# Halves of the K and Q projections placed singly between transposes and products of a batch step

## The reference

```python
x = x + xattn(layernorm(x), ctx, ctx, Wq, Wk, Wv, Wo, bo, g)   # x, ctx: (32, 64, 512)
x = x + ffn(layernorm(x), c1_w, c2_w, w1, w2t)

def xattn(q, k, v, ...):              # per batch, 8 heads of 64
    qh = softmax(Wq q, over the 64 channels of a head) * 64 ** -0.5
    kh = softmax(Wk k, over the 512 positions)
    context = kh vh^T                 # 64 x 64 per head
    out = context^T qh ; out = Wo out + bo ; out = out / norm * g * sqrt(64)

def ffn(x, c1_w, c2_w, w1, w2t):      # per row
    inter = x c1^T c2^T ; per block of 32 of the 1792: idx = argmax
    h = relu(w1[idx] . x) ; out = h w2t[idx]
```

## Time and profile before

| | us |
|---|---|
| median of 3 runs | 860.18 |
| lowest, highest | 857.99, 1524.28 |
| the profiled execution | 858.17 |
| its span, first to last instruction | 856.3 |

### The profile page before, as it was taken

How to read it: one execution, slowest core, us unless ns; L and a number is a source line. 1 busy time by engine, 2 the same in 40 slices (tenths; PEclk the granted TensorE clock), 3 DMA queues, 4 the chain that set the end, 5 groups by cost and what they waited for, 6 DMA issues and landing times. The chain is left out here.

```text
span 856.3 us, 14103 instructions
## 1 busy us (share of the span) xinstructions
PE 803.4 (94%) x4832; PEld 545.6 (64%) x4832; DVE 647.0 (76%) x954; ACT 409.1 (48%) x819; POOL 445.0 (52%) x520
## 2 busy tenths in 40 slices
PE   4999999999999999999947999999999999999998
PEld 2455555555555555555525878787887878788876
DVE  5788888988888888888745676777766777776674
ACT  3688888888788888888721111111111111111111
POOL 5687786787687787787403333343333334433332
PEclk9999999999999999999978999999999999999999
DMA  6223323323323323321220100111111011111000
GB/s 158 75 64 90 91 61 91 90 62 90 90 62 90 90 61 90 90 62 55 69 62 25 38 27 11 38 38 38 38 38 37 2 38 38 38 38 38 13 4 22
DMA packets 30101, 48.07 MB, mean 56 GB/s; under 512 B 4816, under 2 KB 13136, under 8 KB 30032
## 3 DMA queue, kind: packets, MB, share of 16 engines
q1 hardware_dynamic: 29360, 46.19, 18.4%
q10 hardware_dynamic: 672, 0.98, 0.5%
HBM read 38.77 MB, written 8.39 MB: 55 GB/s over the span
## 5 line engine op out<-in xcount | busy, mean ns | idle before, releaser
L637 POOL TENSOR_TENSOR ranked<-mask,rank 128x256 bf16<-128x256 bf16 (+1 forms) x64 | 66.8, 1044 | 198.8 <-DVE mask L788 198.8
L476 PE MATMUL po<-ET,ctxT 128*64 128x512 f32 x256 | 137.0, 618 | 3.1
L479 PE MATMUL po<-QT,G 128*64 128x512 f32 x256 | 136.8, 617 | 0.0
L256 POOL TENSOR_TENSOR Q<-Q,qrec 128x1024 f32<-128x1024 f32 x64 | 120.5, 1905 | 11.6 <-DVE qrec L344 11.5
L711 ACT ACTIVATE hT_hi<-turned 128x256 fp32r<-128x256 f32 (+1 forms) x64 | 34.9, 545 | 188.5 <-PE turned L920 188.5
L304 DVE TENSOR_REDUCE qmax<-slot 128x16 f32<-128x1024 f32 x64 | 78.1, 1220 | 37.7 <-PE slot L528 37.7
L909 PE MATMUL hidden<-weights_hi,xT_hi 128*128 128x512 f32 (+1 forms) x256 | 97.3, 380 | 1.4 <-DVE xT_lo L770 1.4
L909 PE MATMUL hidden<-weights_lo,xT_hi 128*128 128x512 f32 (+1 forms) x256 | 95.2, 372 | 0.0
L909 PE MATMUL hidden<-weights_hi,xT_lo 128*128 128x512 f32 (+1 forms) x256 | 94.7, 370 | 0.0
L933 PE MATMUL acc<-weights_hi,hT_hi 128*128 128x512 f32 x224 | 92.0, 411 | 0.0
L393 ACT ACTIVATE ET<-turn_e 128x512 f32<-128x512 f32 x128 | 76.7, 599 | 31.5 <-PE turn_e L453 31.5
(11 more groups left out here) (98 smaller groups left out, 1623.4 us busy)
## 6 DMA issues: line engine op xcount, KB each, us to landing
c_in<-in_ctx SPq DMA_DIRECT2D x64, 128.0 KB, 2.8
x_in<-in_x SPq DMA_DIRECT2D x64, 128.0 KB, 2.6
stage<-in_ffn_w SPq DMA_DIRECT2D x32, 225.0 KB, 2.9
attn_out<-po_sb SPq DMA_DIRECT2D x32, 128.0 KB, 2.3
attn<-attn_out SPq DMA_DIRECT2D x16, 256.0 KB, 2.8
xr<-in_x SPq DMA_DIRECT2D x16, 256.0 KB, 3.0
out<-result SPq DMA_DIRECT2D x16, 256.0 KB, 2.0
ctxT<-in_ctxT SPq DMA_DIRECT2D x31, 128.0 KB, 2.0
```

The costliest lines, as they stand in the source:

```text
L256: nc.gpsimd.tensor_tensor(half, half, qrec[1 - par][:, s, :].unsqueeze(2).broadcast_to([P, HALF, D]), ALU.mult).then_inc(q_scaled, 1)
L476: nc.tensor.matmul(po[0:C, :], ctxT[1 - par][:, m, :], ET[m % 2][:], start=(m == 0), stop=(m == NT - 1)).then_inc(p_mm, 1)
L479: nc.tensor.matmul(po[C:P, :], G[par][:, m, :], QT[m % 2][:], start=(m == 0), stop=(m == HT - 1)).then_inc(out_mm, 1)
```

## The change

The halves are taken apart. TensorE's order becomes: turn(0), gp, **second half of Q of the batch before**, turn(1), products(0), **first half of K**, turn(2), products(1), **second half of K**, turn(3), products(2), **first half of Q**, products(3). VectorE, ScalarE and GpSimd are reordered with it. No instruction's shape changes, and none is added: VectorE's two `neg_kmax` reductions, which stood together, stand apart.

On TensorE the halves become two functions, called between the rounds:

```diff
+                    def keys(s):
+                        if real(known, 0):
+                            if s == 0:
+                                pe.wait_ge(c_ready, g + 1)
+                                pe.wait_ge(w_lo, 1)
+                            if later(2 * g - 1 + s):
+                                pe.wait_ge(q_shifted, 2 * g - 1 + s)
+                            for n, (w, c) in enumerate(((wk_hi, c_high), (wk_lo, c_high), (wk_hi, c_low))):
+                                for i in range(2):
+                                    j = slice((2 * s + i) * P, (2 * s + i + 1) * P)
+                                    rows = slice(i * C, (i + 1) * C)
+                                    last = nc.tensor.matmul(slot[s][:, i, :], w[rows, j], c[par][rows, :],
+                                                            start=(n == 0), stop=(n == 2))
+                            last.then_inc(k_proj, 1)
+
+                    def queries(b, q, s):
+                        if real(known, b - g):
+                            pe.wait_ge(x_ready, b + 1)
+                            pe.wait_ge(w_lo, 2)
+                            pe.wait_ge(k_exped, 2 * b + s + 1)
+                            for n, (x, w) in enumerate(((x_high[q], wq_hi), (x_high[q], wq_lo), (x_low, wq_hi))):
+                                for i in range(2):
+                                    t = slice((2 * s + i) * P, (2 * s + i + 1) * P)
+                                    rows = slice(i * C, (i + 1) * C)
+                                    last = nc.tensor.matmul(slot[s][:, i, :], x[rows, t], w[rows, :],
+                                                            start=(n == 0), stop=(n == 2))
+                            last.then_inc(q_proj, 1)
+
...
                         last.then_inc(g_mm, 1)
+                    queries(g - 1, 1 - par, 1)
                     turn(1)
                     products(0)
-                    if real(known, 0):
...
+                    keys(0)
                     if known == 0:
                         fold_vo()
-                        pe.wait_ge(w_lo, 2)
                     turn(2)
                     products(1)
+                    keys(1)
                     turn(3)
                     products(2)
+                    queries(g, par, 0)
                     products(3)
-                    if real(known, 0):
...
```

The edits of the other engines:

```diff
-                    if known != 0:
-                        x_rest()
...
-                        pool.wait_ge(stage_loaded[par], 16 * (k + 1))
-                        nc.gpsimd.tensor_copy(weights_hi[:, cols], stage[par][:]).then_inc(stage_hi, 1)
...
-                                                ALU.subtract).then_inc(stage_done, 1)
                     if real(known, 1):
...
                         nc.gpsimd.tensor_tensor(x_bias[1 - par][:], neg_mean[:], rstd[1 - par][:],
...
+                    if known != 0:
+                        x_rest()
+                    if real(known, 0):
...
+                        pool.wait_ge(stage_loaded[par], 16 * (k + 1))
+                        nc.gpsimd.tensor_copy(weights_hi[:, cols], stage[par][:]).then_inc(stage_hi, 1)
...
+                                                ALU.subtract).then_inc(stage_done, 1)
...
                                 krec[:].unsqueeze(2).broadcast_to([P, HT, C]), ALU.mult, ALU.mult)\
                                 .then_inc(g_ready, 1)
 
-                    if real(known, -1):
-
...
+                    def shift_q(s):
+                        if real(known, -1):
                             dve.wait_ge(q_proj, 2 * g - 1 + s)
                             src = heads(slot[s][:])
                             nc.vector.tensor_reduce(qmax[:, s, :], src, AX.X, ALU.max).then_inc(q_max, 1)
...
                                 heads(Q[1 - par][:, 2 * s:2 * s + 2, :]), src,
                                 qmax[:, s, :].unsqueeze(2).broadcast_to([P, HALF, D]),
                                 ALU.subtract).then_inc(q_shifted, 1)
-                            if s == 0:
-                                gains()
...
+
+                    def max_k(s):
+                        if real(known, 0):
+                            dve.wait_ge(k_proj, 2 * g + s + 1)
+                            nc.vector.tensor_reduce(neg_kmax[par][:, 2 * s:2 * s + 2], slot[s][:], AX.X, ALU.max,
+                                                    negate=True).then_inc(k_max, 1)
+
+                    def sum_q(s):
+                        if real(known, -1):
+                            dve.wait_ge(q_exped, 2 * g - 1 + s)
+                            nc.vector.tensor_reduce(qsum[:, s, :], heads(Q[1 - par][:, 2 * s:2 * s + 2, :]),
+                                                    AX.X, ALU.add).then_inc(q_sum, 1)
+                            dve.wait_ge(q_sum, 2 * g - 1 + s)
+
+                            if later(2 * g - 4):
+                                dve.wait_ge(q_scaled, 2 * g - 4)
+                            nc.vector.reciprocal(qrec[1 - par][:, s, :], qsum[:, s, :]).then_inc(q_rec, 1)
+
                     if known == -1:
                         dve.wait_ge(w_in, 16)
                         split_weights(1, wk_hi, wk_lo)
-                    if real(known, 0):
-                        for s in range(2):
...
+                    shift_q(0)
                     if real(known, 1):
                         dve.wait_ge(x_loaded[1 - par], 32 * ((k if par == 0 else k + 1) + 1))
                         nc.vector.bn_stats(stats[:], x_in[1 - par][:])
...
                         split_weights(0, wq_hi, wq_lo)
                     if known == 0:
                         copy_vo()
-                    if real(known, -1):
-                        for s in range(2):
...
+                    gains()
+                    shift_q(1)
+                    sum_q(0)
+                    max_k(0)
+                    sum_q(1)
                     if real(known, -1):
                         dve.wait_ge(k_exped, 2 * g)
                         nc.vector.reciprocal(krec[:], ksum[1 - par][:]).then_inc(k_rec, 1)
+                    max_k(1)
                     if known == B + 1:
                         split_ffn_constants()
 
...
                     copy(0)
                     exp_q(0)
                     copy(1)
+                    if real(known, 1):
+                        act.wait_ge(x_biased, g + 2)
+                        nc.scalar.activation(x_in[1 - par][:], x_in[1 - par][:], ACT.Identity,
+                                             bias=x_bias[1 - par][:], scale=rstd[1 - par][:]).then_inc(x_normed, 1)
                     exp_q(1)
                     copy(2)
                     exp_k(0)
                     copy(3)
                     exp_k(1)
-                    if real(known, 1):
-                        act.wait_ge(x_biased, g + 2)
...
                     if real(known, -1) or real(known, -2):
 
                         rows = slice(0 if real(known, -1) else C, P if real(known, -2) else C)
```

More of the change, by code:

```diff
@@ L320, in step @@
                         split_weights(1, wk_hi, wk_lo)
-                    if real(known, 0):
-                        for s in range(2):
-                            dve.wait_ge(k_proj, 2 * g + s + 1)
-                            nc.vector.tensor_reduce(neg_kmax[par][:, 2 * s:2 * s + 2], slot[s][:], AX.X, ALU.max,
-                                                    negate=True).then_inc(k_max, 1)
+                    shift_q(0)
                     if real(known, 1):
@@ L334, in step @@
                         copy_vo()
-                    if real(known, -1):
[L336 to L342, removed]
-                                dve.wait_ge(q_scaled, 2 * g - 4)
-                            nc.vector.reciprocal(qrec[1 - par][:, s, :], qsum[:, s, :]).then_inc(q_rec, 1)
+                    gains()
[3 more added lines that the diff above has]
+                    sum_q(1)
                     if real(known, -1):
@@ L408, in step @@
                     exp_k(1)
-                    if real(known, 1):
-                        act.wait_ge(x_biased, g + 2)
-                        nc.scalar.activation(x_in[1 - par][:], x_in[1 - par][:], ACT.Identity,
-                                             bias=x_bias[1 - par][:], scale=rstd[1 - par][:]).then_inc(x_normed, 1)
                     if real(known, -1) or real(known, -2):
@@ L494, in step @@
                         last.then_inc(g_mm, 1)
+                    queries(g - 1, 1 - par, 1)
                     turn(1)
                     products(0)
-                    if real(known, 0):
-                        pe.wait_ge(c_ready, g + 1)
-                        pe.wait_ge(w_lo, 1)
-                        for s in range(2):
-                            if later(2 * g - 1 + s):
-                                pe.wait_ge(q_shifted, 2 * g - 1 + s)
-                            for n, (w, c) in enumerate(((wk_hi, c_high), (wk_lo, c_high), (wk_hi, c_low))):
```

(21 more changed lines are left out.)

10 lines of the change are left out of this document (4 added, 6 removed).

## The result

| | before | changed |
|---|---|---|
| median of 4 runs, us | 859.61 | 845.02 |
| lowest, us | 857.99 | 843.26 |
| the profiled execution, us | 858.17 | 845.60 |
| its span, us | 856.3 | 843.7 |

The ratio of the times is 0.983, with an interval of 0.981 to 0.985: faster, by 1.7%, where 844 us and -1.7% were forecast. One of before's four runs took 1524.28 us and is left out of the ratio; the median of the other three is 859.04.

A forecast was written before the change was run, and what follows sets the result against it. A ring over TensorE and VectorE, neither full, was taken to close the step. 30 steps at 12.33 instead of 12.86 gave -15.9 us, start +1.1, end +0.5: -14.3 from 858.17, 844 us; range 835 to 855.

The forecast's parts named there:

- the side of "same": Outcome that the time stays within about 2% of no change; chance 0.53, against 0.40 faster and 0.07 slower.
- The three waits: TensorE's waits at turn(0)'s transposes of Q, second half of K and products(3), about 1.0 us per step, all go.
- A lone half: On TensorE, a half of Q or K standing apart from another half takes 0.90 us, bounds 0.80 and 1.02.
- Splitting costs 0.4 per step: On TensorE, 13 borders between tile shapes instead of 10, at 0.10 us each, with lost pairs: 0.4 us per step.
- The step of 12.33: Attention step on TensorE from turn(0) to turn(0): 12.33 us, where the 30 steps averaged 12.86.
- VectorE's ring at 12.2: Loop from Q(0) through VectorE's list and exp of K(1) to turn(0), then Q(0): 24.42 us over two steps.
- exp of K(1) 0.3 us early: ScalarE's last exp of K ends some 0.3 us before turn(0) needs it, so TensorE stays the bound.
- ScalarE and GpSimd covered: ScalarE's moved normalization finds its bias ready 0.3 us early; GpSimd's 2.94 us wait per step has room for its work.
- The slower rival: ScalarE's normalization waits for GpSimd's bias, delaying the exp of K(1) and turn(0): step 13.68, 884 us; chance 0.07.
- The start, +1.1: ScalarE normalizes x ahead of step 0's exps of K; step 2 begins at 34.0 us: +1.1, bounds 0 and 4.3.
- The end, +0.5: In step 32 the last half of Q comes behind turn(0) and gp; scalings end at 10.4 instead of 9.9: +0.5 us.
- the ring: Old step's loop: VectorE waits for Q's halves, last on TensorE; TensorE's second half of K waits for VectorE's slot.

The follow-up runs named there:

- the version with three groups fewer: Against the changed kernel: products in pairs, Q's halves together at step end, VectorE's K maxima ahead of Q sums, ScalarE's old order; 829.27 us, 0.965 of before.

## Why the prediction was right

The mechanism holds, and nearly every term was met. That the median lies within 1.0 us of the forecast owes something to two errors that offset each other: the attention phase gave 14.9 us where 14.3 was forecast, and the longer half clock, which three of the four executions have by their mean clock, took about 2 back. The change stayed under 2%, the side of "same", to which the prediction gave 0.53.

- **The three waits go** (about 1.0 us per step): right. None is left in the trace. That it takes the orders of both sides together is shown by the halves of the change: with one side alone two of the waits stay (13.24) or one of 3 us forms (17.12). What each of the three is worth alone was not tested.
- **A lone half costs 0.90**: right, also in the two neighbourhoods that no row had: behind gp 0.89, ahead of products 0.91. With one pair put together again the step is 12.13, with the products paired too 11.93. The Trainium skill (TensorEngine Tiling (Array Packing), Key Properties) has a change of tiling mode drain TensorE; the rows fit that, with 0.10 us at each end of a group of halves at full clock, though a drain itself is seen in none.
- **Splitting costs 0.4 per step, against 1.0 of waits**: the step does not rest on this sum, and it is a little off; it would give 12.2. The waits are 0.37 at turn(0), 0.33 at K(1) and 0.28 at products(3) (1.19 for the 0.91 of products ahead of products), 0.98 together. What comes back is 0.40 for the lone halves and 0.10 for products(3), which no longer stands behind products(2): 0.50. The difference is the 0.48 by which the usual step fell, 12.81 to 12.33.
- **The step of 12.33**: measured 12.33. That the mean of 12.86 falls to it, longer steps included, had no reason in the prediction; it is 1.7 of the 16.1 us. Three of the four longer steps were long at the transposes of Q, whose scaling is now over a microsecond early, as the prediction laid out.
- **VectorE's ring at 12.2, exp of K(1) 0.3 us early**: right in place, a little off in size. It is 0.63 early; VectorE works 12.33 - 1.21 = 11.12 us of the step, not 11.35. From a maximum of Q to what follows its subtraction it is 2.40 and 2.39 now, for 2.49 and 2.52 before without the bracket: small gaps of the old step had been counted as work. The exp takes 1.45. The ring stands near 12.0, not 12.2.
- **ScalarE and GpSimd covered**: right, and as thin as told: 0.28 us on ScalarE. The slower rival is real once GpSimd's order goes back.
- **The start, +1.1**: measured +0.65. The exps came at 17.94 (18.3 was forecast) and step 2 at 33.58 (34.0).
- **The end, +0.5**: +0.49; the last scalings start 6.61 after turn(0) of step 32 for 6.13 before, where 6.6 was forecast:

```profile
409.96 3.76 POOL L256 TENSOR_TENSOR Q<-Q,qrec 128x1024 f32<-128x1024 f32 x2 [7.94 <-DVE qrec L329]
```

- **The feed-forward phase at nothing**: right for its work, but the profiled execution gave 2.3 us back there by the clock. The prediction had allowed for a median 2 us above a good execution, without naming the cause.

## What to carry to other kernels

When an engine shows 97% and its neighbour 87%, lay the step out by the distances between starts: what closes the step may be a ring through both. Here the distances gave the new step to 0.01 us before anything was run, as long as the clock stayed full; with a wait of 3 us per step the same layout missed by 1.7. Count the ends of groups of another tile shape as work: breaking the ring paid 0.98 us per step and gave 0.50 back in lone groups, and the version with three groups fewer got 0.40 of that back. A reorder over several engines is one change; take its parts back one at a time, since the gain may hang on one (GpSimd's, 1.14 us per step) while another (ScalarE's) only costs the start.

## What the runs showed of the hardware

- In the kernel with TensorE's order alone TensorE stands 2.97 us in every step of 17 us that was looked at between the first and the last. Directly behind that wait its matmuls kept their full-clock lengths; 2.3 us later four transposes took 1.11 us for 0.66, and in the five steps from 203.80 to 289.31 the granted clock fell to 0.50 and came back to 1.00, 0.90 over 100 us. Shorter waits left it at 1.00: 0.3 to 0.4 us, three times a step, before, and up to 0.92 us with GpSimd's order back.
- After the gap between the phases the half clock held for 17.1 us in six profiled executions and for 27.3 us in four, which makes about 2 us of the time.
- Between starts of matmuls a group of 64-row halves takes 0.10 us more at its entry and 0.10 at its exit when its neighbour has another tile shape (0.33 for 0.23), and nothing between a half of Q and a half of K, which have the same.
